# Local attention with scaled Q, projections three tiles ahead, and the 64-row and 64-column products side by side

## The reference

```python
q = l2norm(q) * qs                    # 8 heads of 64 channels
k = l2norm(k) * ksc
q, k = rotary_xpos(q, k)
bq = q.reshape(b, h, w, WINDOW, d) * QK_SCALE        # WINDOW = 64
sim = einsum('bhwid,bhwjd->bhwij', bq, look_around(bk))
attn = softmax(where(mask, -max, sim))
out = einsum('bhwij,bhwjd->bhwid', attn, look_around(bv))
x = x + out.reshape(...) @ wo
```

## Time and profile before

| what | us |
|---|---|
| median of 3 runs | 1312.03 (1311.81 to 1312.66) |
| profiled execution, its own time | 1309.68 |
| its span on the core | 1307.8 |
| TensorE busy (matmul) | 1153.8, 88% |
| VectorE busy | 915.5, 70% |
| ScalarE busy | 850.6, 65% |
| GpSimd busy | 789.2, 60% |
| share of TensorE in the chain that ended last | 55% |

### The profile page before, as it was taken

The page is one execution under the profiler, slowest core; times in us unless marked ns, Lnnn a source line. Parts: engine busy times, 40 slices in busy tenths (PEclk is TensorE's granted clock), DMA queues, the critical chain, the costliest instruction groups (busy, mean ns, idle before and its releaser), DMA issues.

```text
span 1307.8 us, 36416 instructions
## 1 busy us (share of the span) xinstructions
PE 1153.8 (88%) x12703; PEld 865.5 (66%) x12704; DVE 915.5 (70%) x2475; ACT 850.6 (65%) x2476; POOL 789.2 (60%) x705
## 2 busy tenths in 40 slices
PE   5899898999888999979998989989979985779995
PEld 2576685777755666536766856768569873648985
DVE  6898678887765666769886698878754337774334
ACT  3899858999544455549998589994425543334554
POOL 5888438886456354168873488854377753237772
PEclk8999999999989999989999999999879996978998
DMA  7011100011000000000111000113157650025775
GB/s 222 22 25 28 29 9 20 22 27 26 21 11 3 4 3 3 3 1 18 26 26 29 17 10 22 26 26 93 45 143 220 202 157 26 1 81 160 230 199 154
DMA packets 69808, 78.21 MB, mean 60 GB/s; under 512 B 25094, under 2 KB 50501, under 8 KB 69509
## 3 DMA queue, kind: packets, MB, share of 16 engines
q1 hardware_dynamic: 64133, 64.70, 17.6%
q0 software_dynamic: 5504, 11.28, 3.5%
...
## 4 chain that ended last, share of the span: by engine, by line
PE 55%; DVE 12%; ACT 10%; DMA 8%; POOL 6%; issue 5%; POOLq 1%; SPq 1%; DVEq 0%; ACTq 0%
PE bank L916 5%; PE bank L1846 5%; ACT pB L795 4%; DMA arena<-arena 3%; PE bank L637 3%; PE bank L600 3%; DMA y_rows<-stg,inv_u 3%; PE bank L928 3%; PE bank L1515 3%; PE bank L559 3%; PE bank L545 3%; PE bank L612 3%; PE bank L1536 3%; PE bank L551 3%; POOL arena L2176 2%
## 5 line engine op out<-in xcount | busy, mean ns | idle before, releaser
L864 POOL TENSOR_TENSOR rn<-ss,mhalf 128x16 f32<-128x16 f32 x64 | 187.2, 2924 | 6.8
L2104 DVE SCALAR_TENSOR_TENSOR act_b<-bank,vec,gl 128x128 f32<-128x128 f32 x258 | 75.0, 345 | 133.0 <-ACT gl L1927 112.9
L1846 PE MATMUL bank<-arena 128*128 128x128 f32 x1032 | 135.5, 282 | 1.6 <-issue 1.6
L1846 PEld LDWEIGHTS bank<-arena 128*128 128x128 f32 x1032 | 126.1, 197 | 6.2 <-issue 5.3
L795 ACT ACTIVATE pA<-bank,nb,rn 128x128 f32<-128x128 f32 x256 | 113.5, 484 | 3.0 <-DVE nb L726 3.0
L795 ACT ACTIVATE pB<-bank,nb,rn 128x128 f32<-128x128 f32 x256 | 113.3, 478 | 1.7 <-DVE nb L726 1.7
L850 POOL TENSOR_TENSOR arena<-arena 128x512 f32<-128x512 f32 x64 | 81.5, 1274 | 46.0 <-DVE nb L726 34.9
L1927 ACT ACTIVATE gl<-bank,vec 128x128 f32<-128x128 f32 x258 | 76.0, 365 | 51.1 <-PE bank L1846 36.0
L857 POOL TENSOR_TENSOR arena<-arena 128x512 f32<-128x512 f32 x64 | 81.3, 1271 | 43.1 <-DVE arena L689 16.4
L1609 DVE TENSOR_REDUCE act_b<-bank 128x2 f32<-128x512 f32 x128 | 79.5, 684 | 39.6 <-PE bank L1491 39.6
L2182 POOL DMA_INDIRECT y_rows<-stg,inv_u x86 | 84.6, 983 | 35.0 <-issue 18.6
...
## 6 DMA issues: line engine op xcount, KB each, us to landing
...
```

The source lines that it names most:

```text
L864: pool.tensor_tensor(rn[:, q % 4, :, :], ss[:, 1, :].rearrange("p (a h) -> p a h", a=2), mhalf[:, :].rearrange("p (a h) -> p a h", a=2), A ...
L1846: m = pe.matmul(bank[q % 2][:, j * P:(j + 1) * P], we1[q][:, half * HR + j * P:half * HR + (j + 1) * P], xT[:, q, :], start=True, stop=True)
```

## The change

- Q is scaled like K: GpSimd multiplies Q's sum (`qadd`) by the norm factors into `qr` (`q_scaled`). `exps` takes no scale any more, and its bias is the maximum itself; `nb8` and its two products are gone.
- Q's sum is split: VectorE adds the first 256 columns (`q_sum` of `lo_dve`), GpSimd the other 256.
- `qr` and `kr` have two buffers; `rn` has two instead of four.
- TensorE projects three tiles ahead instead of two. A projection waits for `square` of the tile before instead of `rope`, since `rope` now comes first and `square` second.
- In TensorE's step both transposes of the probabilities stand ahead of `sims`, and `pv` directly behind it.
- The steps of ScalarE, VectorE and GpSimd are ordered anew, and so are the calls that prepare tiles 0 to 2.

```diff
@@ -202,13 +202,13 @@
-        qr = cut(10240, INNER)
+        qr = [cut(n, INNER) for n in (10240, 12288)]
+        qadd = cut(11776, INNER)
         kadd = cut(10752, INNER)
-        kr = cut(11264, INNER)
+        kr = [cut(n, INNER) for n in (11264, 12800)]
         ss = sb("ss", [P, 2, 16])
-        rn = sb("rn", [P, 4, 2, 8])
+        rn = sb("rn", [P, 2, 2, 8])
         mx8 = sb("mx8", [P, 2, 2, 4])
-        nb8 = sb("nb8", [P, 2, 2, 4])
...
@@ -541,13 +541,13 @@
                 if n:
-                    pe.wait_ge(s.rk_ab, n)
+                    pe.wait_ge(s.sqk_done, 2 * n - 1)
...
                 if n:
-                    pe.wait_ge(s.rq_ab, n)
+                    pe.wait_ge(s.sqk_done, 2 * n)
...
@@ -653,19 +653,19 @@
-                if has(2):
-                    k_proj(q + 2)
-                    q_proj(q + 2)
+                if has(3):
+                    k_proj(q + 3)
+                    q_proj(q + 3)
                 if has(-1):
                     turn(q - 1, 0)
+                if has(-2):
+                    out_proj(q - 2)
+                if has(1):
+                    q_turn(q + 1)
+                if has(-1):
+                    turn(q - 1, 1)
                 if has(0):
                     sims(q)
-                if has(-1):
-                    turn(q - 1, 1)
-                if has(1):
-                    q_turn(q + 1)
-                if has(-2):
-                    out_proj(q - 2)
                 if has(-1):
                     pv(q - 1)
                 if has(0):
@@ -681,9 +681,11 @@
             def rope(q, k):
                 n = tb + q
                 bank = (BQ, BK)[k]
-                dve.wait_ge(s.sqk_done, 2 * n + 2 - k)
+                dve.wait_ge((s.q_ps, s.k_ps)[k], n + 1)
                 if n:
-                    dve.wait_ge((s.qr_ready, s.kadd_ready)[k], n)
+                    dve.wait_ge((s.qadd_ready, s.kadd_ready)[k], n)
+                    if k == 0:
+                        dve.wait_ge(s.qd_ready, n)
...
@@ -721,11 +723,19 @@
-                for x in range(2):
-                    dve.wait_ge(s.mx_ready, 2 * n + x + 1)
-                    dve.tensor_tensor(nb8[:, par, x, :], mx8[:, par, x, :],
-                                      rn[:, q % 4, 0, :].rearrange("p (u x) -> p x u", x=2)[:, x, :], ALU.mult)\
-                        .then_inc(s.smax_ready, 1)
+
+            def q_sum(q):
+                n = tb + q
+                dve.wait_ge(s.rq_ab, n + 1)
+                if n:
+                    dve.wait_ge(s.qr_ready, n)
+                if n == 2 * NT:
+                    dve.wait_ge(s.a_strip, 4 * NBATCH)
+                dve.tensor_tensor(qadd[:, 0:SEQ], rab[:, 0, 0:SEQ], rab[:, 1, 0:SEQ], ALU.add).then_inc(s.qd_ready, 1)
+
+            def sums(q):
+                squares(q)
+                q_sum(q)
 
...
@@ -736,29 +746,33 @@
-                if has(-3):
-                    result(q - 3)
-                if has(1):
-                    rope(q + 1, 0)
-                    squares(q + 1)
+                if has(3):
+                    rope(q + 3, 1)
                 if has(-1):
-                    norm(q - 1, 0)
                     norm(q - 1, 1)
-                if has(2):
-                    rope(q + 2, 1)
+                if has(3):
+                    rope(q + 3, 0)
+                if has(-2):
+                    result(q - 2)
                 if has(0):
                     maxima(q)
-
-            return LoDve(step, rope, squares)
+                if has(3):
+                    squares(q + 3)
+                if has(0):
+                    norm(q, 0)
+                if has(3):
+                    q_sum(q + 3)
+
+            return LoDve(step, rope, sums)
         def lo_act(act, l, pb):
             tb = pb * NT
 
             def square(q, k):
                 n = tb + q
-                if k == 1 and n:
+                if n:
                     act.wait_ge(s.ssk_raw, n)
-                act.wait_ge((s.q_ps, s.k_ps)[k], n + 1)
+                act.wait_ge((s.rq_ab, s.rk_ab)[k], n + 1)
...
@@ -787,14 +801,13 @@
-                act.wait_ge(s.smax_ready, 2 * n + x + 1)
...
                 for u in range(4):
                     m = act.activation(pr[:, u * P:(u + 1) * P], BS[x][:, u * P:(u + 1) * P], ACT.Exp,
-                                       bias=nb8[:, par, x, u:u + 1], scale=rn[:, q % 4, 0, 2 * u + x:2 * u + x + 1],
-                                       accum_out=den8[:, par, x, u:u + 1])
+                                       bias=mx8[:, par, x, u:u + 1], accum_out=den8[:, par, x, u:u + 1])
...
@@ -809,24 +822,25 @@
-                if has(2):
-                    square(q + 2, 0)
                 if has(-2):
                     o_out(q - 2)
                 if has(-1):
-                    pt_out(q - 1, 1)
+                    v_out(q - 1)
+                    exps(q - 1, 1)
+                if has(0):
+                    qk_out(q, 1)
+                if has(-1):
+                    pt_out(q - 1, 0)
+                if has(3):
+                    square(q + 3, 1)
                 if has(1):
                     qk_out(q + 1, 0)
+                if has(-1):
+                    pt_out(q - 1, 1)
+                if has(3):
+                    square(q + 3, 0)
                 if has(0):
                     exps(q, 0)
-                    exps(q, 1)
-                if has(1):
-                    qk_out(q + 1, 1)
-                if has(3):
-                    square(q + 3, 1)
-                if has(0):
-                    v_out(q)
-                    pt_out(q, 0)
 
             return LoAct(step, square, qk_out)
...
@@ -853,31 +867,41 @@
                 n = tb + q
                 pool.wait_ge(s.rq_ab, n + 1)
                 if n:
-                    pool.wait_ge(s.qT_ps, n)
-                pool.tensor_tensor(qr[:, :], rab[:, 0, :], rab[:, 1, :], ALU.add).then_inc(s.qr_ready, 1)
+                    pool.wait_ge(s.qr_ready, n)
+                pool.tensor_tensor(qadd[:, SEQ:INNER], rab[:, 0, SEQ:INNER], rab[:, 1, SEQ:INNER], ALU.add)\
+                    .then_inc(s.qadd_ready, 1)
+
+            def q_scaled(q):
+                n = tb + q
+                pool.wait_ge(s.qd_ready, n + 1)
+                pool.wait_ge(s.qadd_ready, n + 1)
+                pool.wait_ge(s.rn_ready, n + 1)
+                if n > 1:
+                    pool.wait_ge(s.qT_ps, n - 1)
+                pool.tensor_tensor(heads(qr[q % 2]), heads(qadd[:, :]),
+                                   bc(rn[:, q % 2, 0, :].unsqueeze(2), [P, LH, LD]), ALU.mult).then_inc(s.qr_ready, 1)
 
             def power(q):
...
-                if q > 3:
-                    pool.wait_ge(s.exp_done, 2 * n - 6)
-                pool.tensor_tensor(rn[:, q % 4, :, :], ss[:, 1, :].rearrange("p (a h) -> p a h", a=2),
...
+            def sums(q):
+                k_sum(q)
+                q_sum(q)
+
+            def scaled(q):
+                q_scaled(q)
+                k_scaled(q)
+
             def step(q):
-                def has(d):
-                    return 0 <= q + d < NT
-
-                if has(0):
-                    k_scaled(q)
-                if has(1):
-                    if q:
-                        pool.wait_ge(s.smax_ready, 2 * (tb + q))
-                    k_sum(q + 1)
-                    q_sum(q + 1)
-                    power(q + 1)
-
-            return LoPool(step, k_sum, q_sum, power)
+                if 0 <= q + 3 < NT:
+                    sums(q + 3)
+                    power(q + 3)
+                    scaled(q + 3)
+
+            return LoPool(step, sums, power, scaled)
@@ -1152,11 +1181,13 @@
             lo1.k_proj(1)
             ff0(7)
-            lo1.q_turn(0)
             lo1.q_proj(1)
             ff0(8)
+            lo1.q_turn(0)
+            lo1.k_proj(2)
+            ff0(9)
+            lo1.q_proj(2)
             lo1.k_turn(0)
-            ff0(9)
             for q in range(NT):
                 lo1.step(q)
@@ -1233,19 +1269,23 @@
             lo1.rope(0, 0)
-            lo1.squares(0)
+            lo1.sums(0)
             ff0(7)
             lo1.rope(1, 1)
+            lo1.rope(1, 0)
             ff0(8)
+            lo1.sums(1)
+            lo1.rope(2, 1)
+            lo1.rope(2, 0)
+            lo1.sums(2)
             for q in range(NT - 1):
                 lo1.step(q)
@@ -1296,21 +1336,20 @@
-            for j in range(5):
+            for j in range(6):
                 ff0(j)
             lo1.square(0, 1)
-            ff0(5)
+            ff0(6)
             lo1.square(0, 0)
-            ff0(6)
             ff0(7)
             act.preload_act_table(ACT.Exp)
             lo1.square(1, 1)
+            lo1.square(1, 0)
+            ff0(8)
             lo1.qk_out(0, 0)
-            ff0(8)
-            lo1.square(1, 0)
+            lo1.square(2, 1)
             ff0(9)
-            lo1.qk_out(0, 1)
-            lo1.square(2, 1)
+            lo1.square(2, 0)
             for q in range(NT):
```

(2 more changed lines are left out.)

76 lines of the change are left out of this document (44 added, 32 removed).

## The result

The changed kernel takes 1333.88 us (median of 4, 1329.73 to 1337.98); in the same session the kernel before took 1311.92 (median of 4). The ratio is 1.0166, 95% interval 1.0141 to 1.019: slower, where 1330.0 was forecast. The profiled execution took 1336.53 (span 1334.6).

A forecast was written before the change was run, and what follows sets the result against it. TensorE bounds the steady tiles before; VectorE's 7.90 us circle takes over. Per pass, +6.2 at the last logits and -1.7 at the end give +4.5, +18 over four passes: 1327.7 profiled, 1330.0 forecast, range 1318 to 1344.

The forecast's parts named there:

- The steady tile: Local attention's repeating tile after the change: 7.90 us between mask products for tiles 2 to 12, 7.49 for the last three.
- VectorE's circle: Chain of waits through VectorE's queue, from one tile's maxima to the next's: 7.90 us, the longest of three.
- TensorE's 7.78: TensorE's work per tile: 7.93 us less 0.15 for one saved change of array shape.
- ScalarE's 7.49: Latency chain of a tile through logits, maxima, exponentials, second normalisation and transposes: 7.49 us, pacing the last three tiles.
- The start: Start of a pass: tile 1's logits wait for GpSimd's powers and sums, K's rotation and a normalisation; cost 7.0 us.
- The interior, 109.4: Logits of tile 1 to last logits in a pass: 11 intervals of 7.90 us and 3 of 7.49.
- The end, 8.3: End of a pass: last logits to `pv(15)` takes 8.3 us instead of 9.98, no longer held by the DMA; -1.7.
- The sum: Start, interior and end together: +4.5 us a pass, alike for all four passes, +18 in all.
- (a): Rival: scale pointer costs nothing, exponentials stay 0.44 us, ScalarE's circle is 8.23; 5.8 a pass more, 1353 us; 7%.
- (b): Rival: VectorE and GpSimd collide, 0.9 us a tile lands in the 7.90 circle, +40, 1370 us; 10%.
- (c): Rival: faster, TensorE's 7.6 us tile sets the pace, fill mostly hidden (3.5), under the end's 1.7; 1303 us; 15%.
- (d): Rival: errors cancel, VectorE's circle 7.7 us, fill 5, end gains 1.7; 0.3 a pass, 1313 us; 6%.

The follow-up runs named there:

- the first version with a lead of two: Changed kernel's scaled Q, two buffers, pointerless exponentials and split Q sum, with the kernel before's two-tile lead and TensorE and ScalarE orders; ratio 0.9965 to the kernel before.

## Why the prediction was right, by its own steps

**The steady tile: right.** 7.90 forecast, 7.82 found, odd and even alike, and VectorE's circle it is: a longer sum on VectorE, and none on GpSimd, lengthened the tile (0.24 for 0.29). The terms for the half sum (0.34) and the last stretch through TensorE (0.64, 1.36) came out, and so did GpSimd's multiplies (1.04); the sum of squares with what follows took 1.53 for 1.58, the second normalisation 0.88 for 0.93. GpSimd's half took 0.73 for 0.63.

**TensorE's 7.78: right in its term, too long as a sum.** The saved change of shape is worth 0.15, as taken. But 7.93 was the longer of two alternating tiles, the other takes 7.80, and by the estimate above the changed kernel's own TensorE work is 7.72 and 7.67. TensorE is thus 0.10 to 0.15 behind VectorE's circle. It changes nothing in the forecast, since the 7.90 stood above either.

**ScalarE's 7.49: too short by 0.15.** In the last three tiles it is 7.65. The step that failed is "from there through `turn(q, 1)` to the next logits 0.64". `q_turn` stands ahead of those transposes and waits for K's copy, which ScalarE makes only after all eight exponentials:

```profile
327.95 0.63 PE L567 MATMUL bank<-ident_sb,arena 128*128 128x128 f32 x4 [0.46 <-ACT arena L798]
```

The path runs through that copy and eight transposes, not through the multiply. In the last of the three intervals there is no `q_turn`; the second half's transposes wait there for the copy of the first half (`pt_out`, L790), and the interval is again 7.65.

**The start: the mechanism right for three passes, its size 7.0 too small.** Found are 6.9, 8.5, 9.5 and 8.9. In the second pass the chain holds link by link: with the lag of 3.6 taken off, tile 2's power starts at 212.6 where 212.3 was forecast, and the first 0.3 is all that is missing until K's sum of tile 3. Behind it the forecast leaves out a collision (K's sum 1.82 for 1.27) and TensorE's lower clock (the transposes 1.04 for 0.66), and tile 1's logits come at 223.1 for 221.6. Without the first three powers the last logits of the last pass come 16.8 earlier. The first pass's 6.9 is close to 7.0 by luck: its chain is VectorE's queue, and replacing the powers leaves it as it was. Taking the second pass's chain for all four was the step that failed there.

**The interior, 109.4: right in part by luck.** Found are 109.0 to 110.2. The steady intervals are shorter than forecast (7.82 for 7.90), the last three longer (7.65 for 7.49), and in three passes the second interval is 1.1 to 1.3 longer than the others, at TensorE's lower clock, which the forecast had nowhere. **The end, 8.3: right.** It is 8.3 in three passes and 9.6 in the second, where the last transposes ran at the lower clock. No `pv` waited for V's rows.

**The sum.** +4.5 a pass was forecast, 3.6 to 8.0 found, +24 in all in the profiled execution for +18. The starts make 5.8 of the 6 that were missed. The profiled execution lost another 3 in the unchanged attention, which the forecast had at nothing. By the medians it is +22.

**The rivals.** (a) is refuted by the pointer's own 0.09 a piece. (b) did not happen in the steady tile, but is real: the changed kernel has it in the start of a pass, and the tile is 8.48 when the powers go and 8.1 to 8.2 in the first version with a lead of two. (c) failed at its condition, a fill under 1.7 us. (d) failed on both its terms: VectorE's circle is 7.82 and not 7.7, the fill 6.9 to 9.5 and not 5.
